# A selective-state-space stage of a four-layer network: GpSimd makes one of every four input products of the states, from a copy of B that ScalarE takes out of PSUM

## The reference, cut to what matters

```python
dt = jax.nn.softplus(dt + dt_proj_b[None, :, None])
A = -jnp.exp(A_log)
...
def step(state, inp):
    d, b, c, u = inp
    dA = jnp.exp(d[..., None] * A)
    state = state * dA + (d * u)[..., None] * b[:, None, :]
    y = jnp.einsum('bdn,bn->bd', state, c)
    return (state, y)
```

## Time and profile before

| what | us |
|---|---|
| median of 3 runs (lowest, highest) | 1162.64 (1160.04, 1165.0) |
| the profiled execution, its own time | 1156.74 |
| its span, first to last instruction | 1155.3 |
| the units, from the first input product to the last gating | 31.3 to 181.6 |

### The profile page before, as it was taken

How to read it: one execution, slowest core, us unless ns; L and a number is a source line. 1 busy time by engine, 2 the same in 40 slices (tenths; PEclk the granted TensorE clock), 3 DMA queues, 4 the chain that set the end, 5 groups by cost and what they waited for, 6 DMA issues and landing times.

```text
span 1155.3 us, 14112 instructions
## 1 busy us (share of the span) xinstructions
PE 1021.8 (88%) x4772; PEld 701.6 (61%) x4772; DVE 742.0 (64%) x1808; ACT 481.9 (42%) x1158; POOL 257.5 (22%) x206
## 2 busy tenths in 40 slices
PE   5766778999999999999999999999989998987556
PEld 2222233568999998899856555656656765544444
DVE  4888995235666668666755465558757765477653
ACT  3554352136666665666611111125545452132331
POOL 2445562121111112111100011811732100010110
PEclk9887889999999999999999999999999899989677
DMA  5000001001110131110012221111000003211200
GB/s 214 0 1 0 0 1 46 1 28 42 42 42 28 45 117 42 42 42 28 1 42 69 81 69 55 55 55 42 1 1 2 1 1 119 83 41 28 80 19 18
DMA packets 16335, 46.90 MB, mean 41 GB/s; under 512 B 2300, under 2 KB 3462, under 8 KB 15624
## 3 DMA queue, kind: packets, MB, share of 16 engines
q1 hardware_dynamic: 15400, 44.67, 11.6%
q10 hardware_dynamic: 864, 1.34, 0.3%
HBM read 44.96 MB, written 1.05 MB: 40 GB/s over the span
## 4 chain that ended last, share of the span: by engine, by line
PE 73%; DVE 8%; POOL 4%; issue 3%; ACT 2%; POOLq 0%; DVEq 0%; ACTq 0%
PE psum L1409 15%; PE psum L1428 7%; PE psum L906 5%; PE psum L1098 5%; PE psum L1109 5%; PE psum L1078 4%; PE psum L1652 4%; PE psum L767 4%; PE psum L909 3%; PE psum L1089 2%; PE psum L1951 2%; PE psum L930 2%; POOL arena L393 2%; PE psum L778 2%; PE psum L1935 2%
## 5 line engine op out<-in xcount | busy, mean ns | idle before, releaser
L1409 PE MATMUL psum<-xT,arena 128*128 128x512 f32 x400 | 183.4, 601 | 7.6 <-DVE arena L1600 1.9
L1409 PEld LDWEIGHTS psum<-xT,arena 128*128 128x128 f32 x400 | 75.4, 192 | 85.0 <-issue 83.2
L988 POOL TENSOR_TENSOR arena<-arena,mhalf 128x8 f32<-128x8 f32 x32 | 53.5, 1672 | 274.1 <-DVE arena L973 274.1
L1494 DVE TENSOR_TENSOR arena<-psum,arena 128x512 f32<-128x512 f32 x50 | 34.5, 691 | 110.0 <-PE psum L1409 110.0
L1463 ACT ACTIVATE arena<-psum 128x512 f32<-128x512 f32 x50 | 29.7, 596 | 174.6 <-PE psum L1409 174.6
L393 POOL TENSOR_TENSOR arena<-arena 128x512 f32<-128x512 f32 x64 | 82.5, 1311 | 79.0 <-DVE arena L695 76.2
L1210 DVE SCALAR_TENSOR_TENSOR X<-psum,arena,X 128x256 f32<-128x256 f32 x128 | 55.9, 478 | 68.0 <-PE psum L1109 68.0
L1428 PE MATMUL psum<-arena 128*128 128x256 f32 x400 | 95.2, 380 | 2.7 <-DVE arena L1494 2.7
L450 PE MATMUL psum<-arena,ident 128*128 128x512 f32 x128 | 77.6, 703 | 22.5 <-POOL arena L393 22.3
L1428 PEld LDWEIGHTS psum<-arena 128*128 128x128 f32 x400 | 75.3, 190 | 32.1 <-issue 21.4
L1506 DVE SCALAR_TENSOR_TENSOR X<-psum,arena,X 128x256 f32<-128x256 f32 x192 | 83.2, 478 | 8.5 <-PE psum L1428 8.1
(11 more groups left out here) (279 smaller groups left out, 1981.2 us busy)
## 6 DMA issues: line engine op xcount, KB each, us to landing
arena<-in_moe SPq DMA_DIRECT2D x50, 384.0 KB, 3.0
arena<-in_w SPq DMA_DIRECT2D x32, 384.0 KB, 3.0
arena<-in_w SPq DMA_DIRECT2D x2, 1024.0 KB, 6.7
arena<-in_gu SPq DMA_DIRECT2D x1, 1280.0 KB, 6.3
X<-in_x SPq DMA_DIRECT2D x2, 512.0 KB, 9.7
arena<-in_ctok SPq DMA_DIRECT2D x2, 512.0 KB, 7.1
arena<-in_fsideT SPq DMA_DIRECT2D x1, 1024.0 KB, 4.8
arena<-in_fside SPq DMA_DIRECT2D x1, 1024.0 KB, 6.9
```

The lines of the kernel that those rows point to most:

```text
L1409: mm = nc.tensor.matmul(bank[b], m.W[:, slot, which, c * P:(c + 1) * P], k.xT[:, c, cols], start=c == 0, stop=c == DC - 1)
```

## The change

In the odd units (s % 2 == 1, `shared_out`) the input product of block 1 moves from VectorE to GpSimd. GpSimd cannot take B from where it lies, so ScalarE first copies it from PSUM bank 0 to a new SBUF buffer `Bs` (one for all units); VectorE's remaining product of such a unit waits for that copy too, though it still reads PSUM. In GpSimd's queue the product of unit s+1 stands ahead of the two products with C of unit s. TensorE's rows of the next unit wait for the copy and for VectorE's product. A third buffer of input products is added, so that the one GpSimd writes is used by odd units only.

```diff
+def shared_out(s):
+    return s % 2 == 1
+
+def input_of(m, s, c):
+    return m.dBu[:, c + c * (s % 2), :]
...
     for s in range(m.UNITS):
+        if s + 1 < m.UNITS and shared_out(s + 1):
+            pool.wait_ge(*at("Bs", s + 1))
+            pool.wait_ge(*at("DU", (s + 1) // m.NSTATE))
+            if s:
+                pool.wait_ge(*at("scan", s - 1, 1))
+            nc.gpsimd.tensor_tensor(input_of(m, s + 1, 1), m.DU[:, (s + 1) // m.NSTATE, 1, :], m.Bs,
+                                    ALU.mult).then_inc(*tick("dBu_p", s + 1))
         for c in range(m.NI):
             pool.wait_ge(*at("scan", s, c))
...
             if s:
-                pe.wait_ge(*(at("dBu", s - 1, 1) if b == m.bank_B else at("Cs", s - 1)))
+                if b == m.bank_C:
+                    pe.wait_ge(*at("Cs", s - 1))
+                elif shared_out(s - 1):
+                    pe.wait_ge(*at("dBu", s - 1, 0))
+                    pe.wait_ge(*at("Bs", s - 1))
+                else:
+                    pe.wait_ge(*at("dBu", s - 1, 1))
...
         h, n = s // NSTATE, s % NSTATE
+        if shared_out(s):
+            act.wait_ge(*at("B_ps", s))
+            if s >= 2:
+                act.wait_ge(*at("dBu_p", s - 2))
+            nc.scalar.copy(m.Bs, bank[m.bank_B]).then_inc(*tick("Bs", s))
         act.wait_ge(*at("C_ps", s))
...
-        for c in range(NI):
-            dve.wait_ge(*at("B_ps", s))
+        for c in range(1 if shared_out(s) else NI):
+            dve.wait_ge(*(at("Bs", s) if shared_out(s) else at("B_ps", s)))
...
-            dve.wait_ge(*at("dBu", s, c))
+            dve.wait_ge(*(at("dBu_p", s) if c and shared_out(s) else at("dBu", s, c)))
```

More of the change, by code:

```diff
@@ L327, in __init__ @@
         self.gate = k.place(NT, S)
-        self.dBu = k.place(NI, HALF)
+        self.dBu = k.place(3, HALF)
+        self.Bs = k.place(HALF)
         self.Hs, self.HC = k.place(4, HALF), k.place(4, HALF)
@@ L509, in mamba_pe @@
     turned(1)
-    k.free[0], k.free[1] = [("dBu", m.UNITS - 1, 1)], [("Cs", m.UNITS - 1)]
+    k.free[0], k.free[1] = [("dBu", m.UNITS - 1, 0), ("Bs", m.UNITS - 1)], [("Cs", m.UNITS - 1)]
     k.free[2], k.free[3] = [("scan", m.UNITS - 1, 0)], [("scan", m.UNITS - 1, 1)]
@@ L683, in mamba_dve @@
         dve.wait_ge(*at("DU", h))
-        for c in range(NI):
-            dve.wait_ge(*at("B_ps", s))
+        for c in range(1 if shared_out(s) else NI):
+            dve.wait_ge(*(at("Bs", s) if shared_out(s) else at("B_ps", s)))
             if s:
                 dve.wait_ge(*at("scan", s - 1, c))
-            nc.vector.tensor_tensor(m.dBu[:, c, :], m.DU[:, h, c, :], bank[m.bank_B],
+            nc.vector.tensor_tensor(input_of(m, s, c), m.DU[:, h, c, :], bank[m.bank_B],
                                     ALU.mult).then_inc(*tick("dBu", s, c))
@@ L691, in mamba_dve @@
             dve.wait_ge(*at("dA", s, c))
-            dve.wait_ge(*at("dBu", s, c))
+            dve.wait_ge(*(at("dBu_p", s) if c and shared_out(s) else at("dBu", s, c)))
             if s >= 2:
                 dve.wait_ge(*at("HC", s - 2, c))
-            nc.vector.tensor_tensor_scan(m.Hs[:, 2 * (s % 2) + c, :], bank[m.bank_dA[c]], m.dBu[:, c, :],
+            nc.vector.tensor_tensor_scan(m.Hs[:, 2 * (s % 2) + c, :], bank[m.bank_dA[c]], input_of(m, s, c),
                                          0.0, ALU.mult, ALU.add).then_inc(*tick("scan", s, c))
```

## The result

The changed kernel takes 1174.19 us (median of 19 executions) against 1161.1 for the kernel before (19 executions beside it). The ratio is **1.0088, with a 95% interval of 1.0068 to 1.0108**: slower by about 10 us. The single executions of the changed kernel spread from 1163 to 1176 us, those of the kernel before from 1159 to 1165. The profiled execution took 1167.72 us, with a span of 1166.4; that of before 1156.74.

The account below looks back on a forecast made before the run. VectorE looked like the bound (busy 137.2 of 150.4 us in the units); after the change, a ring across engines. Pairs at full clock +3.1 us and clock falls +6.7 give +9.8 on the median 1162.64: 1172.4 us, range 1157 to 1184.

Parts of the forecast that it names:

- The ring: Loop GpSimd product, products with C, TensorE add, B matmul, ScalarE copy: 7.07 us per pair of units, 0.23 longer than before.
- VectorE's share: VectorE's own work in a pair of units after losing one product: 6.37 us, 0.47 less than 6.84.
- The five pairs with other work on VectorE: Pairs where VectorE has extra work and stays the bound: each gains 0.47 us, together -2.3 us.
- rival 3: GpSimd's extra product also collides with VectorE steps having both inputs in SBUF: up to +9.2 us more, 1181.6 us; chance 0.10.
- The other eight: Remaining pairs of units run at the ring's beat at full clock: 8 x 0.23, +1.8 us.
- The three with work on TensorE behind an add: Pairs after units 3, 12 and 22: later adds delay the next B by about 1.2 us each, +3.6 us.
- the skip term: TensorE work after unit 12: VectorE's 2.70 us idle for the following B taken as showing the add's delay already on the path.
- The clock term: TensorE's clock drops behind 2.3 us pauses in the units, 1.11 us per pair: six pairs, +6.7 us, bounds 0 to 12.2.
- reaches the end in full: After the units the dense layer's matmuls follow at once in TensorE's queue, so the units' gain or loss carries through unchanged.
- The weighed rule: Skill's rule that only single long idle gaps endanger TensorE's clock: the pauses would pass and the sum stop at +3.1 us.
- Rival 1: VectorE still sets the pair, 0.47 us gained in each: 1155.1 us, at best 1153.3; chance 0.12.
- Rival 2: The ring sets the pair at full clock, pauses of 2.3 us leaving the clock alone: +3.1 us, 1165.7 us; chance 0.18.

Follow-up runs that it names:

- e1: Changed kernel with GpSimd's input product placed between its two products with C instead of ahead of both; ratio 1.0020 to the kernel before, pair 6.43 us.
- e2: Changed kernel with TensorE's add of block 0 moved one iteration later, GpSimd's order kept; ratio 0.9965 to the kernel before, pair 6.43 us.
- e4: Changed kernel, but GpSimd's product goes to an unread buffer and VectorE makes all four; ratio 1.0124 to the kernel before, pair 7.04 us.
- e3: Kernel before plus only ScalarE's copy of B in odd units and the waits for it; ratio 1.0011 to the kernel before, pair 6.85 us.
- e11: Changed kernel unmodified, one more single traced execution; 1168.5 us, units 156.2 us.
- e7: Kernel before plus five useless VectorE additions between the last scan and the last gating; ratio 1.0080 to the kernel before, units 152.1 us.
- e6: Kernel before with only TensorE's add of block 0 moved one iteration later; ratio 0.9939 to the kernel before, units 142.5 us, pair 6.85 us.

## Why the prediction was right or wrong, point by point

**The direction and the size** were right: 1172.4 forecast, 1174.19 measured, within the range. In part that is luck: two terms of the sum had the wrong size, and a cost that it did not have made up for them.

**The ring** was right in every link: 7.07 us forecast, 7.05 measured; the pause of TensorE 2.3 forecast, 2.17 measured; GpSimd's product 1.27 forecast, 1.268 measured. Two independent cuts (e1, e2) bring the beat to 6.43, where VectorE's share of 6.37 was forecast, and restoring VectorE's work (e4) leaves it at 7.05. The copy is free (e3).

**Pair by pair** the three kinds were each mis-sized. The five pairs with other work on VectorE were to give 0.47 each, -2.3; they gave -1.2 (+0.7, -1.4, 0.0, -0.1 and -0.4). The first lost 0.7, because VectorE's normalisation ran 1.1 us longer beside GpSimd. In units 9 to 11 steps of the softplus grew as well (L626 of before from 0.86 to 1.18 us, L639 from 1.39 to 1.71). That is rival 3's mechanism, and the normalisation has one SBUF tensor as input, so I had looked for it in the wrong steps. The other eight were to cost 1.8 and cost 5.0; 1.1 and 1.3 of that lie in the pairs of units 14 and 26, where the lower clock level holds for a while in the changed kernel and not in before, 1.2 in the pair of unit 20. The three with work on TensorE behind an add were to cost 3.6; they cost 0.4, as the sum of +2.9 after unit 3 and -1.6 and -0.9 after units 12 and 22. After unit 3 the clock falls in four traces of the changed kernel. In e11 it did not, and that pair cost 1.3, near the 1.2 forecast. The timeline of the changed kernel there:

```profile
49.01 1.13 PE L474 MATMUL psum<-arena,ident 128*128 128x512 f32 x2 [2.17 <-POOL arena L411]
49.98 3.36 PE L433 MATMUL psum<-arena 128*128 128x512 f32 x4
53.13 0.85 PE L468 MATMUL psum<-arena 96*128 96x512 bf16 x2
53.80 1.28 DVE L717 TENSOR_TENSOR arena<-arena,psum 128x512 f32<-128x512 f32 x2 [3.23 <-PE psum L468]
```

At the skip term I had misread. The four matmuls that take 3.62 us there run at the lower level; the timeline of the changed kernel has them at the upper one:

```profile
107.42 1.88 PE L439 MATMUL psum<-arena 128*128 128x512 f32 x4
...
109.56 1.28 DVE L717 TENSOR_TENSOR arena<-arena,psum 128x512 f32<-128x512 f32 x2 [1.54 <-PE psum L468]
```

So 1.74 of the 2.70 us for which VectorE waited in before were the clock, and the add ahead of them was slow too (2.08 against 1.12). The row did not show that the queue's order was on the path at full clock. In e7, with the queues of before, the same wait was 1.30. After unit 22 the changed kernel takes 7.60 us in all its traces, and before's queues took 7.45 at the upper level (e7) and 8.49 at the lower: the price of the order there is 0.15, not 1.2.

**The clock term** is the step that failed: "I take about half, 6 pairs: +6.7", all in the units, and all on top of what before had. The mechanism is real. In the last eight units, where before is at the upper level throughout, all five traces of the changed kernel have the clock fall behind a pause of 2.17, once in four of them and twice in e11; none of the eight traces without the ring has a fall there. The timeline of the changed kernel:

```profile
158.29 1.12 PE L474 MATMUL psum<-arena,ident 128*128 128x512 f32 x2 [2.16 <-POOL arena L411]
159.26 0.86 PE L468 MATMUL psum<-arena 96*128 96x512 bf16 x2
159.91 3.35 PE L474 MATMUL psum<-arena,ident 128*128 128x512 f32 x4
```

The four instructions of two adds take 3.35, where at 175.17 above they take 2.19, and the pair of unit 26 takes 8.17 in place of 7.05: 0.9 to 1.2 us more in four traces, near the 1.11 forecast, and 2.7 more in e11. Wrong was the number of such pairs. In the last eight units it was one of four, in e4, with the same ring, none, and elsewhere the changed kernel was at the upper level where before was not. Between the first scan and the last gating the lower level holds for 44.2 us before and 41 us in three traces of the changed kernel, 48 and 52 in the others. Falls moved more than they multiplied. The units cost 4 to 5 us, once 7.1, where the sum had 9.8.

**What the sum left out** is the clock outside the units. The text took it for granted that what the units lose "reaches the end in full", and no more. e7 shows that a delay can cost more than itself, through TensorE's clock in what follows. For the changed kernel the traces do not show where: they come from executions of 1164.6 to 1168.5 us, while ten of the nineteen lie above 1174. But the granted clock of every execution is on record. It was 0.937 to 0.939 in those ten and 0.942 to 0.949 in the other nine; before had 0.947 in the median of the 25 executions timed beside e1, and never less than 0.941. As the lower level is half of the upper, a mean of 0.938 over 1175 us is 146 us at the lower level, 0.947 over 1160 is 123; the 23 us between them, at 0.42 each, are some 10 us, an estimate from the table above. At the same clock, 0.941 or 0.942, before took 1163.8 to 1165.0 us and the changed kernel 1169.6 to 1171.5. So about 6 us are there at an equal clock, and the rest goes with a lower one. In which stages the longer executions of the changed kernel lose it, and why they should more often than before's, is open.

**The weighed rule** of the Trainium skill ("TensorE: Matmul & The Clock Gate", section "HAM oscillation — how this bites in real kernels"), by which only long single pauses would matter: the traces do not agree. The clock fell behind pauses of 2.17 us that are no long idle gap of that rule's kind. With the rule alone the sum would have been +3.1, against 4.1 to 4.6 in the units of four traces and 7.1 in e11.

**The rivals.** Rival 1 (VectorE sets the pair) is what e1 and e2 look like, and even then the product earned nothing that could be measured over e6. Rival 2's number was nearest for the units alone, but its condition did not hold: the pauses did not leave the clock alone.

## What to carry to other kernels

Before moving work to an idle engine, follow one lap from the new instruction through every queue that it stands in; here no engine was over its share, yet a float32 add that waited for GpSimd stood in front of the matmul that feeds the copy. Look first at what stands behind a waiting instruction: moving TensorE's adds one iteration later in the kernel before, without moving any work, gave 0.61% (e6, 7 us), about what the change could have given at best (7.5 us, if all sixteen pairs had gained). And a difference of under 1% needs traces of several executions, for a single trace can place half of it in a stage that the change does not touch.

## What the runs showed of the hardware

The same instructions after the units took 973.7 to 985.3 us in fourteen traces, and the time went with the time that TensorE's clock was at its lower level in them, 64.9 to 92.2 us. In the second attention the same work followed the same pause of 4.61 us with the lower level held for 3.4 us in one execution and 17.1 in another, a difference of 5.8 us in time. Inside the ring the clock fell behind single pauses of 2.17 us that came once in 7.05. VectorE's normalisation, one SBUF tensor in and SBUF out, took 3.48 us beside three GpSimd multiplications and 2.38 beside two; of its single instructions those that began 0.1 us behind the start of a GpSimd multiplication took 1.35 us, one alone 0.40.
